# Level-zero products from the keys themselves, one product for the rows' first values, and a new order of the work

## The chip, the cores and the metric

The kernel runs on one core of a Trainium2 chip. The metric is the device time of one launch, in microseconds; three runs of the kernel before gave 5051.2 us in the median (5048.74 to 5053.33).

## The reference, cut to what matters

A macaron block: half a feed-forward layer, an attention-like layer with a delta rule, half a feed-forward layer again, each on normalised inputs and added to the input. The change touches the middle layer only, for 8 sequences of 256 tokens, 16 heads, 4 keys and values per token, chunks of 64 tokens in the reference:

```python
w = bg[..., None] * kg
Mi = [einsum('bhtsd,bhsmd->bhtsm', kg[:, :, :, i, :][:, :, :, None, :] * Dts, w) for i in range(Rr)]
M = tril(stack(Mi, axis=3).reshape(b, h, C * Rr, C * Rr), k=-1)
kexp = kg * exp(Gg)[:, :, :, None, :]
rhs = (vg - einsum('bhtid,bhdv->bhtiv', kexp, S)).reshape(...)
u = solve_triangular(M, rhs, lower=True, unit_diagonal=True)
o = SCALE * (o_inter + o_intra)          # from q exp(G) S and attn u
S_new = exp(glast)[..., None] * S + einsum('bhtid,bhtiv->bhdv', kdec, u)
```

Here `Dts` is exp of a difference of cumulated log decays, `kdec` the keys times the decay to the chunk's end. Keys, queries and values come from projections, a causal convolution of 4 taps and silu.

## The kernel before, in words

Everything is float32. After the first feed-forward phase come 64 head steps (4 tiles of 512 tokens, 16 heads); each holds two sequences' halves (`hb` 0 and 1) of 8 chunks `c` of 32 tokens with 4 keys each, 128 rows per chunk. The work of one head step is spread over about four turns of one loop: in turn `p` every engine works on steps `p+1` (projections), `p`, `p-1`, `p-2` (inverse and recurrence) and `p-3` (output). In the texts here `s0` is step `p`, `s1` is `p-1`, and so on, and `sn` is `p+1`. Each engine has its own list of calls, written out by hand, and runs it strictly in that order; a call first waits on semaphores that say its operands are there and its target is empty. PSUM banks 0 and 1 go round among projections, turns, norm, gate, decay and output (`bank_use`), the accumulators `acc` among the convolutions (`acc_use`).

The parts of a step:

- `project_k(s, 0..4)` (4 keys and the query) and `project_v(s, 0..3)` on TensorE; `tap_*` (ScalarE) and `conv_*` (VectorE, three taps) into `acc`; `silu_*` (ScalarE) into `KQ` and `V`. `decay`, `softplus`, `add_up` (a scan, L1437), `distance` and `factors` (ScalarE, exponentials F0, Fl, Fe) make the decay factors.
- `products(s, q, l)` for four groups `q` of 16 token blocks: the products of keys with keys and queries, split by level `l` of a binary tree so that the decay factors never overflow. `levels(s, q, l)` on VectorE (L1394) makes X = KQ times Fl for levels 1 to 4, `level(s, q)` on GpSimd (L1769, L1770) makes X0 for level 0: a copy of the 40 columns of KQ and 20 more columns times F0. All levels 0 to 2 of a group go to bank 2, levels 3 and 4 to bank 3. `evacuate` (VectorE, L1479 and L1485) empties bank 2 into Pd, `keep` (ScalarE) bank 3 into E and At.
- `take`, `norm`, `weigh` (VectorE) lay the first 32 by 32 blocks out; `begin` on GpSimd (L1778, L1784) clears LZ and puts the first values of the rows in with four instructions, `rows` (L1796, L1799) solves 31 rows by 62 instructions, each behind the one before. `unfold` and `turn` on VectorE, `first` to `fourth` on TensorE with copies on ScalarE join the blocks to the inverse Ztf.
- `spread` on GpSimd (L1739) makes kexp and kdec, `query` (L1758) qn; `turn` on TensorE (L810) transposes kdec, `turn_v` (L801) V.
- The recurrence over chunks, both halves interleaved: `rhs` on TensorE, `rhs` on VectorE (Rs, L1397), `solve` on TensorE, `solve` on ScalarE (Us), `update` on TensorE (kdT, At, qn), `update` on VectorE (S), and again. Then `out_square`, `mean_square`, `out_root`, `gated`, `output`.

All products go through one helper (L739), VectorE's through L1394 and L1397, ScalarE's through L1056 and L1057, so the trace is read by tiles.

Of the kernel before, what the change touches and what calls it, by code (L numbers as in the profile page):

```python
# [12 lines left out]
P = 128  # L13
# [13 lines left out]
C_SEL = C_SMALL + 6  # L27
# [64 lines left out]
def build(nc, x, out, wkq, wv, wo, vec, wf1, wg1, wb, bg1, wu, wd, fvec, wsd, cst, B, H):  # L92
# [4 lines left out]
    with ctx:  # L97
# [24 lines left out]
        half_c = [cs[:, C_SEL + 16 + half:C_SEL + 17 + half] for half in range(2)]  # L122
# [436 lines left out]
        X0 = sb("X0", [P, 16, 60])  # L559
# [16 lines left out]
        LZ = sb("LZ", [P, 32, 16])  # L576
# [35 lines left out]

        g_zero, g_kdec, g_kexp, g_qn, g_copy, g_X0, g_init, g_row = (sem(f"g_{n}") for n in ("zero", "kdec", "kexp", "qn", "copy", "X0", "init", "row"))

        def turns(order, count):
# [10 lines left out]
            ("k", 3, 0, v_ck, 15, 11), ("ms", 0, 3, a_ms, 3, 0), ("k", 4, 0, v_ck, 15, 14),  # L628
            ("gate", 0, 1, a_gate, 1, 0), ("out", 0, 3, v_out, 2, 0), ("v", 2, 1, v_cv, 12, 8),
            ("v", 3, 1, v_cv, 12, 11), ("out", 1, 3, v_out, 2, 1), ("vturn", 0, 2, a_vt, 4, 0),  # L630
            ("vturn", 1, 2, a_vt, 4, 1), ("turn", 0, 1, a_kdT, 4, 0), ("vturn", 2, 2, a_vt, 4, 2),
            ("vturn", 3, 2, a_vt, 4, 3), ("k", 0, -1, v_ck, 15, 2), ("norm", 0, 0, a_qs, 1, 0),
            ("turn", 1, 1, a_kdT, 4, 1), ("k", 1, -1, v_ck, 15, 5), ("k", 2, -1, v_ck, 15, 8),
            ("turn", 2, 1, a_kdT, 4, 2), ("turn", 3, 1, a_kdT, 4, 3), ("v", 0, 0, v_cv, 12, 2),
            ("decay", 0, -1, v_sp, 1, 0), ("v", 1, 0, v_cv, 12, 5),
        ], 2)
        acc_use = turns([
            ("k", 3, 0, a_k, 5, 3), ("k", 4, 0, a_k, 5, 4), ("v", 2, 1, a_v, 4, 2),
            ("v", 3, 1, a_v, 4, 3), ("k", 0, -1, a_k, 5, 0), ("k", 1, -1, a_k, 5, 1),
            ("k", 2, -1, a_k, 5, 2), ("v", 0, 0, a_v, 4, 0), ("v", 1, 0, a_v, 4, 1),  # L640
# [94 lines left out]
        def delta_tensor(e):  # L735
# [216 lines left out]
            for p in range(-1, NS + 3):  # L952
                project_k(p, 3)
                solve(p - 3, 1, 7)
                update(p - 3, 0, 7)
                update(p - 3, 1, 7)
                mean_square(p - 3)
# [10 lines left out]
                products(p - 1, 2, 0)  # L968
                products(p - 1, 2, 1)
                first(p - 2, 0)  # L970
                products(p - 1, 2, 2)
                second(p - 2, 0)
                products(p - 1, 2, 3)
                output(p - 3, 1)
# [5 lines left out]
                turn_v(p - 2, 2)  # L980
                products(p - 1, 2, 4)
                turn_v(p - 2, 3)
                first(p - 2, 1)
                project_k(p + 1, 0)
                second(p - 2, 1)
                products(p - 1, 3, 0)
                total(p)
# [4 lines left out]
                solve(p - 2, 0, 0)  # L992
                third(p - 2, 1)
                turn(p - 1, 1)
                update(p - 2, 0, 0)
                fourth(p - 2, 1)
                project_k(p + 1, 1)
                solve(p - 2, 1, 0)
                rhs(p - 2, 0, 1)
                project_k(p + 1, 2)  # L1000
# [4 lines left out]
                products(p, 0, 0)  # L1005
                rhs(p - 2, 0, 2)
                solve(p - 2, 1, 1)
                products(p, 0, 1)
                turn(p - 1, 2)
                solve(p - 2, 0, 2)  # L1010
                update(p - 2, 1, 1)
                rhs(p - 2, 1, 2)
                update(p - 2, 0, 2)
                products(p, 0, 2)
                solve(p - 2, 1, 2)
                rhs(p - 2, 0, 3)
                update(p - 2, 1, 2)
                solve(p - 2, 0, 3)
                rhs(p - 2, 1, 3)
                update(p - 2, 0, 3)  # L1020
                solve(p - 2, 1, 3)
                rhs(p - 2, 0, 4)
                update(p - 2, 1, 3)
                turn(p - 1, 3)
                solve(p - 2, 0, 4)
                project_v(p, 0)
                rhs(p - 2, 1, 4)
                update(p - 2, 0, 4)
                solve(p - 2, 1, 4)
                decay(p + 1)  # L1030
                rhs(p - 2, 0, 5)
                update(p - 2, 1, 4)
                products(p, 0, 3)
                solve(p - 2, 0, 5)
                rhs(p - 2, 1, 5)
                products(p, 0, 4)
                solve(p - 2, 1, 5)
                update(p - 2, 0, 5)
                rhs(p - 2, 0, 6)
                update(p - 2, 1, 5)  # L1040
                rhs(p - 2, 1, 6)
                solve(p - 2, 0, 6)
                solve(p - 2, 1, 6)
                update(p - 2, 0, 6)
                update(p - 2, 1, 6)
                rhs(p - 2, 0, 7)
                project_v(p, 1)
                solve(p - 2, 0, 7)
                rhs(p - 2, 1, 7)

        def delta_scalar(e):
# [252 lines left out]
            for p in range(-1, NS + 3):  # L1304
                silu_v(p - 1, 0)
                solve(p - 3, 1, 7)
                tap_k(p, 3)
                out_square(p - 3)
                e.preload_act_table_set("natural_log_exp_and_others")
# [15 lines left out]
                tap_v(p - 1, 3)
                first(p - 2, 0)
                second(p - 2, 0)
                silu_v(p - 1, 2)
                silu_k(p, 4)
                third(p - 2, 0)  # L1330
                turned_v(p - 2, 0)
                turned_v(p - 2, 1)
                square(p)
                turned(p - 1, 0)
                fourth(p - 2, 0)
                turned_v(p - 2, 2)
                turned_v(p - 2, 3)
                rhs(p - 2, 0, 0)
                silu_v(p - 1, 3)
                first(p - 2, 1)  # L1340
                keep(p - 1, 2)
                tap_k(p + 1, 0)
                second(p - 2, 1)
                e.preload_act_table_set("natural_log_exp_and_others")
                factors(p, 0)
                solve(p - 2, 0, 0)
                keep(p - 1, 3)
                third(p - 2, 1)
                turned(p - 1, 1)
                excess(p)  # L1350
                factors(p, 1)
                length(p - 1, 0)
                fourth(p - 2, 1)
                update(p - 2, 0, 0)
                rhs(p - 2, 1, 0)
                tap_k(p + 1, 1)
# [565 lines left out]
```

## Time and profile before

| | |
|---|---|
| median of three runs | 5051.2 us |
| profiled execution | 5064.96 us, its span 5063.2 us |
| TensorE busy | 4653.1 us, 92% |
| VectorE, ScalarE, GpSimd busy | 78%, 66%, 63% |
| mean granted clock of TensorE | 0.946 |
| matmuls | 63328 records (two for each float32 product) |

Busy time is how long at least one instruction of the engine was on its way; for TensorE the end of a product is modelled, and products overlap, so the time from one start to the next says more of its work than the busy share. A granted clock of 1.00 is 2.4 GHz, 0.50 is 1.2 GHz. In the rows, a bracket after a row gives the idle time of the engine ahead of it and what ended it. Weight loads have rows of their own (PEld).

### The profile page before, as it was taken

To read this page: it belongs to the slowest core of one execution; us is meant where nothing else is said; L and a number is where in the kernel's file an instruction comes from. 1 tells how busy PE (TensorE), PEld (TensorE's weight loads), DVE (VectorE), ACT (ScalarE), POOL (GpSimd) and SP (SyncE) were. 2 spreads that over 40 slices of the span, in tenths; PEclk is the share of its full clock that TensorE was granted. 3 is DMA by queue.
4 is the path that set the end of the run, shared out by engine and by line. 5 is a ranking of instruction groups with operands and counts; after the bars stand their busy time and mean duration, and the time that the engine had idled before them with its cause. 6 is when DMAs were issued, how large, how long until landed. Compare 5 with 4: busy or idle time off the path is not lost.

```text
span 5063.2 us, 151418 instructions
## 1 busy us (share of the span) xinstructions
PE 4653.1 (92%) x63328; PEld 3247.3 (64%) x63328; DVE 3967.3 (78%) x7070; ACT 3357.1 (66%) x6641; POOL 3179.8 (63%) x5380
## 2 busy tenths in 40 slices
PE   8869999999999999999999999999999999999889
PEld 5436666666666666666666666666666666666655
DVE  3278888888878888888888888888888888888522
ACT  2267777767767777767677767777677777677421
POOL 0047667767767676777667767677776677676600
PEclk9989999999999999999999999999999999999769
DMA  2110000000000000000100000000000000000010
GB/s 87 62 49 23 25 25 25 13 25 25 33 20 25 29 25 25 25 13 25 33 31 29 14 25 25 25 25 16 27 29 25 25 16 22 25 25 9 3 45 18
DMA packets 49722, 135.45 MB, mean 27 GB/s; under 512 B 7056, under 2 KB 28176, under 8 KB 48400
## 3 DMA queue, kind: packets, MB, share of 16 engines
q1 hardware_dynamic: 49040, 125.77, 7.1%
q8 instruction: 499, 8.18, 0.7%
q14 instruction: 183, 1.50, 0.1%
HBM read 111.60 MB, written 14.16 MB: 25 GB/s over the span
## 4 chain that ended last, share of the span: by engine, by line
PE 60%; DVE 25%; ACT 9%; issue 5%; POOL 1%; DMA 1%; SPq 0%; DVEq 0%; ACTq 0%
PE bank L739 50%; DVE X L1394 9%; PE bank L261 7%; DVE acc L1397 7%; ACT o L1057 2%; PE bank L810 2%; DVE S L1397 1%; DVE o L1397 1%; DVE Pd L1479 1%; DVE x1m L1394 1%; PE bank L801 1%; DVE Zc L1558 1%; DVE C L1437 1%; ACT Ztf L1056 1%; ACT Fl L1057 1%
## 5 line engine op out<-in xcount | busy, mean ns | idle before, releaser
L1397 DVE SCALAR_TENSOR_TENSOR acc<-bank,vc,acc 128x510 f32<-128x510 f32 (+2 forms) x1728 | 1272.3, 742 | 157.9 <-ACT acc L1056 134.9
L1799 POOL TENSOR_TENSOR LZ<-LZ,LT 128x120 f32<-128x120 f32 (+26 forms) x1984 | 958.4, 483 | 155.4
L1394 DVE TENSOR_TENSOR X<-KQ,Fl 128x640 f32<-128x640 f32 x1024 | 1011.4, 1013 | 15.2 <-ACT Fl L1057 15.1
L1796 POOL TENSOR_TENSOR LT<-LA,LZ 128x120 f32<-128x120 f32 (+26 forms) x1984 | 845.2, 426 | 145.8
L1056 ACT ACTIVATE Us<-bank 128x128 f32<-128x128 f32 x1024 | 282.2, 276 | 864.7 <-PE bank L739 852.4
L1769 POOL COPY X<-KQ 128x640 f32<-128x640 f32 x256 | 184.3, 720 | 993.6 <-ACT F L1057 664.8
L739 PEld LDWEIGHTS bank<-X 128*32 128x32 f32 x32768 | 535.9, 115 | 362.3 <-issue 219.8
L739 PE MATMUL bank<-X 128*32 128x60 f32 (+1 forms) x32768 | 648.4, 209 | 127.4 <-DVE Pd L1479 96.3
L739 PE MATMUL bank<-xnTm,WK 128*128 128x512 f32 x1280 | 658.9, 640 | 30.3 <-DMA WK<-in_wkq 13.8
L739 PE MATMUL bank<-xnTm,WV 128*128 128x512 f32 x1024 | 492.7, 605 | 10.6 <-DVE acc L1397 5.1
L739 PE MATMUL bank<-Rs,Ztf 128*128 128x128 f32 x2048 | 458.8, 306 | 36.4 <-ACT Rs L1056 18.3
L1397 DVE SCALAR_TENSOR_TENSOR Rs<-V,knT,bank 128x128 f32<-128x128 f32 x896 | 309.8, 346 | 215.7 <-PE bank L739 208.2
L1739 POOL TENSOR_TENSOR kdec<-KQ,Fe 128x512 f32<-128x512 f32 x256 | 353.4, 1380 | 197.9 <-PE bank L810 197.8
L739 PEld LDWEIGHTS bank<-Rs,Ztf 128*128 128x128 f32 x2048 | 328.3, 193 | 208.0 <-issue 74.1
L1056 ACT ACTIVATE acc<-bank,vc 128x512 f32<-128x512 f32 x576 | 393.8, 684 | 65.8 <-PE bank L739 62.5
L739 PE MATMUL bank<-S,kexp 128*128 128x128 f32 x1792 | 396.6, 304 | 21.9 <-DVE S L1397 0.8
L739 PE MATMUL bank<-Us,kdT 128*128 128x128 f32 x1792 | 384.6, 297 | 16.1
L739 PEld LDWEIGHTS bank<-xnTm,WK 128*128 128x128 f32 x1280 | 228.2, 198 | 266.0 <-issue 185.8
L1739 POOL TENSOR_TENSOR kexp<-KQ,Fe 128x512 f32<-128x512 f32 x256 | 382.0, 1503 | 0.0
L739 PEld LDWEIGHTS bank<-S,kexp 128*128 128x128 f32 x1792 | 283.9, 193 | 118.7 <-DVE S L1397 83.2
L739 PE MATMUL bank<-qn,S 128*128 128x32 f32 x1792 | 352.0, 279 | 0.0
L1397 DVE SCALAR_TENSOR_TENSOR S<-S,egl,bank 128x128 f32<-128x128 f32 x768 | 262.7, 342 | 96.5 <-PE bank L739 92.7
(145 smaller groups left out, 9341.0 us busy)
## 6 DMA issues: line engine op xcount, KB each, us to landing
WK<-in_wkq SPq DMA_DIRECT2D x64, 704.0 KB, 5.6
WV<-in_wv SPq DMA_DIRECT2D x64, 576.0 KB, 4.2
WO<-in_wo SPq DMA_DIRECT2D x64, 128.0 KB, 2.0
wuh<-in_wu SPq DMA_DIRECT2D x2, 1024.0 KB, 7.3
xt<-in_x SPq DMA_DIRECT2D x4, 512.0 KB, 6.4
wuh_d<-wuh SPq DMA_DIRECT2D x1, 2048.0 KB, 6.3
x_d<-x SPq DMA_DIRECT2D x4, 512.0 KB, 3.1
xnT_d<-xT SPq DMA_DIRECT2D x4, 512.0 KB, 2.7
```

What stands on the lines that cost most here:

```text
L261: return e.matmul(o, l, r, start=start, stop=stop, skip_group_check=True)
L739: return e.matmul(o, l, r, start=start, stop=stop, skip_group_check=True)
L801: ins = e.transpose(o[:, P * c:P * c + P], V[:, s % 2, 4 * q + c, :], ident)
L810: ins = e.transpose(o[:, P * c:P * c + P], kdec[:, c, :], ident)
L1056: return e.activation(o, i, f, scale=scale)
L1057: return e.activation(o, i, f, bias=bias, scale=scale)
L1394: return e.tensor_tensor(o, a, b, op)
L1397: return e.scalar_tensor_tensor(out=o, in0=a, scalar=sc, in1=b, op0=op0, op1=op1)
L1739: return e.tensor_tensor(o.rearrange("p u (g i t) -> p (u g) i t", g=4, i=R), KQ[:, s % 2, 16 * q:16 * q + 16, 0:R, :], f.unsqueeze(2).bro ...
L1769: e.tensor_copy(X0[:, :, 0:40], kk.rearrange("p g i t -> p g (i t)")).then_inc(g_copy, 1)
L1796: e.tensor_tensor(tmp, LA[:, j + 1:32, 8 * (j % R) + j // R].unsqueeze(2).broadcast_to([P, rr, cc]), LZ[:, j, 0:cc].unsqueeze(1).broadcast ...
L1799: e.tensor_tensor(LZ[:, j + 1:32, 0:cc], LZ[:, j + 1:32, 0:cc], tmp, SUB).then_inc(g_row, 1)
```

## The change

Three edits, and a new order on four engines.

1. `products(s, q, 0)` reads keys and queries from KQ: a product of the 32 key columns with the 40 columns of keys and queries, and one of the same keys with the 20 scaled columns of X0. X0 has 20 columns per block instead of 60, the copy in `level` goes, and `products` waits for silu of all five blocks.
2. `begin` writes the rows' first values with one instruction, through a view of LZ (`LZd`) and a product with a two-column mask.
3. The order of calls of all four engines is another one, with the bank and accumulator rounds that follow from it; the loop's start is cut at another place, so calls that stood at its end for `p-2` now stand at its start for `p-3`.

```diff
-        half_c = [cs[:, C_SEL + 16 + half:C_SEL + 17 + half] for half in range(2)]
+        half_c = cs[:, C_SEL + 16:C_SEL + 18]
...
-        X0 = sb("X0", [P, 16, 60])
+        X0 = sb("X0", [P, 16, 20])
...
-        LZ = sb("LZ", [P, 32, 16])
+        LZt = sb("LZ", [P, 8 * 66])
+        LZ = LZt[:, 0:512].rearrange("p (r c) -> p r c", c=16)
+        LZd = LZt[:, :].rearrange("p (t x) -> p t x", x=66)[:, :, 0:64].rearrange("p t (h y) -> p t h y", y=32)[:, :, :, 0:18:17]
...
                     w.wait_ge(a_E, nth(s, 8, 2 * q - 1))
+                    w.wait_ge(a_k, every(s, 5))
                     w.wait_ge(g_X0, nth(s, 4, q))
...
-                            ins = mm(o[:, 0:60], X0[:, gb + g, 0:32], X0[:, gb + g, :])
+                            kg = KQ[:, s % 2, 16 * q + gb + g]
+                            mm(o[:, 0:40], keys(kg), kg.rearrange("p i t -> p (i t)"))
+                            ins = mm(o[:, 40:60], keys(kg), X0[:, gb + g, :])
...
-                e.tensor_copy(X0[:, :, 0:40], kk.rearrange("p g i t -> p g (i t)")).then_inc(g_copy, 1)
-                e.tensor_tensor(X0[:, :, 40:60].rearrange("p g (i t) -> p g i t", t=4), kk[:, :, :, 1:8:2],
+                e.tensor_tensor(X0[:, :, :].rearrange("p g (i t) -> p g i t", t=4), kk[:, :, :, 1:8:2],
                                 f.unsqueeze(2).broadcast_to([P, 16, 5, 4]), MUL).then_inc(g_X0, 1)
...
-                flat = LZ[:, :, :].rearrange("p r c -> p (r c)")
-                for k in range(2):
-                    for hf in range(2):
-                        a = 32 * hf + 17 * k
-                        e.tensor_scalar(flat[:, a:a + 463:66], Cn[:, :, 2 * hf + k], half_c[hf], None,
-                                        MUL).then_inc(g_init, 1)
+                e.tensor_tensor(LZd, Cn[:, :, :].rearrange("p t (h k) -> p t h k", h=2),
+                                half_c.unsqueeze(1).unsqueeze(3).broadcast_to([P, 8, 2, 2]), MUL).then_inc(g_init, 1)
```

The new lists, shortened (one entry per call, `3,0` for arguments after the step; `update(s3,1,5)` is `update(p - 3, 1, 5)`).

```
TensorE: update(s3,1,5) solve(s3,0,6) project_k(s0,3) rhs(s3,1,6) update(s3,0,6) solve(s3,1,6) rhs(s3,0,7)
 update(s3,1,6) solve(s3,0,7) products(s1,0,3) rhs(s3,1,7) project_v(s1,1) solve(s3,1,7) update(s3,0,7)
 update(s3,1,7) products(s1,0,4) mean_square(s3) project_k(s0,4) products(s1,1,0..2) gate products(s1,1,3..4)
 output(s3,0) project_v(s1,2) project_v(s1,3) products(s1,2,0) first(s2,0) products(s1,2,1..2) second(s2,0)
 output(s3,1) products(s1,2,3) third(s2,0) turn_v(0) turn_v(1) fourth(s2,0) turn(s1,0) turn_v(2) first(s2,1)
 turn_v(3) products(s1,2,4) second(s2,1) total(s0) project_k(sn,0) solve(s2,0,0) products(s1,3,0..4) turn(s1,1)
 third(s2,1) project_k(sn,1) update(s2,0,0) fourth(s2,1) rhs(0,1) turn(s1,2) solve(1,0) solve(0,1) update(1,0)
 update(0,1) rhs(1,1) project_k(sn,2) rhs(0,2) solve(1,1) solve(0,2) update(1,1) update(0,2) rhs(1,2) rhs(0,3)
 solve(1,2) solve(0,3) update(1,2) products(s0,0,0) rhs(1,3) update(0,3) turn(s1,3) rhs(0,4) solve(1,3)
 project_v(s0,0) products(s0,0,1) solve(0,4) update(1,3) update(0,4) rhs(1,4) decay(sn) rhs(0,5) solve(1,4)
 solve(0,5) update(1,4) products(s0,0,2) rhs(1,5) update(0,5) solve(1,5) rhs(0,6)
VectorE: rhs(s3,0,6) update(1,5) softplus(s0) rhs(1,6) update(0,6) levels(s1,1,1) rhs(0,7) update(1,6) conv_k(s0,3,2)
 levels(s1,1,2) rhs(s3,1,7) conv_k(3,1) conv_k(3,0) levels(s1,1,3) conv_v(1,2) conv_v(1,1) evacuate(s1,0,0)
 conv_v(1,0) evacuate(0,1) levels(1,4) evacuate(0,2) evacuate(0,3) lengths gated(0) gated(1) conv_k(4,2..0)
 evacuate(1,0) unfold(0) unfold(1) evacuate(1,1) turn evacuate(1,2) output(s3,0) evacuate(1,3) levels(2,1..3)
 conv_v(2,2..0) conv_v(3,2..0) output(s3,1) add_up(s0) levels(2,4) levels(3,1) levels(3,2) evacuate(2,0)
 evacuate(2,1) levels(3,3) evacuate(2,2) distance(1) evacuate(2,3) levels(3,4) distance(2) conv_k(sn,0,2)
 conv_k(0,1) evacuate(3,0) conv_k(0,0) evacuate(3,1..3) take conv_k(1,2) norm(0) conv_k(1,1) rhs(s2,0,1) norm(1)
 conv_k(1,0) norm(2) weigh distance(3) ... (recurrence with conv_k(sn,2), levels(s0,0,.), conv_v(s0,0))
GpSimd: begin(s2) rows(s2,0) rows(4) level(s1,1) rows(8) .. rows(28) spread(s1,0,0) spread(0,1) level(s1,2) level(s1,3)
 spread(1,1) query(s1) spread(2,1) spread(1,0) spread(3,1) spread(2,0) level(s0,0) spread(3,0)
```

(`spread(q,0)` makes kdec, `spread(q,1)` kexp.) Before, GpSimd's list after `begin` was `rows(0)`, `rows(4)`, `spread(3,0)`, `rows(8)`, `level(1)`, `rows(12)` to `rows(28)`, `level(2)`, and so on; TensorE had `products(3,0..4)` ahead of the first `solve`, `products(0,4)` inside the recurrence; VectorE had `levels(2,4)`, `(3,1)`, `(3,2)`, `(3,3)` in a row, then three evacuations, `add_up`, `levels(3,4)` and the fourth evacuation. ScalarE's list changes in the same way; `silu_k(sn,0)` moves ahead of `factors(3)`, and there are four calls that load the table of exponentials in a turn instead of three.

## Rows read from the trace of the kernel before

**Rows 1.** The page: busy us and shares, and the chain that ended last.
```profile
PE 4653.1 (92%) x63328; PEld 3247.3 (64%) x63328; DVE 3967.3 (78%) x7070; ACT 3357.1 (66%) x6641; POOL 3179.8 (63%) x5380
...
PE 60%; DVE 25%; ACT 9%; issue 5%; POOL 1%; DMA 1%; SPq 0%; DVEq 0%; ACTq 0%
```
**Rows 2.** Scan L1437 (first, last start); windows: us, busy PE PEld DVE ACT POOL, PEclk.
```profile
L1437 DVE TENSOR_TENSOR_SCAN C<-cs,sp_t x64: 1212/1217/1400, 275.3 to 4674.9; 128x512 f32<-128x512 f32 x64
...
2081.02:2148.99 67.97, 63.32 (x970) 45.12 (x970) 60.75 (x108) 50.40 (x102) 50.48 (x84) 1.00 0.07 24
...
676.00:680.00 4.00, 3.71 (x101) 2.05 (x103) 3.02 (x6) 2.08 (x4) 1.44 (x2) 0.57 0.00 0
```
**Rows 3.** TensorE in order of time: start us, us, instruction; work by start to start.
```profile
2096.18 0.63 PE L739 MATMUL bank<-X 128*32 128x60 f32 x32
2096.74 0.49 PE L739 MATMUL bank<-S,kexp 128*128 128x128 f32 x2
...
2100.31 0.45 PE L739 MATMUL bank<-X 128*32 128x20 f32 x32
2100.69 0.49 PE L739 MATMUL bank<-Rs,Ztf 128*128 128x128 f32 x2
...
2117.56 1.88 PE L739 MATMUL bank<-xnTm,WV 128*128 128x512 f32 x4
2119.28 0.39 PE L739 MATMUL bank<-Rs,Ztf 128*128 128x128 f32 x2
2119.50 0.39 PE L739 MATMUL bank<-S,kexp 128*128 128x128 f32 x2
...
2127.90 2.03 PE L739 MATMUL bank<-X 128*32 128x60 f32 x128 [0.19 <-issue]
2129.86 1.13 PE L739 MATMUL bank<-fgm,WV 128*128 128x512 f32 x2
```
**Rows 4.** Windows of the two stretches of one step, columns as in rows 2.
```profile
2086.26:2122.65 36.39, 35.30 (x345) 27.30 (x342) 30.37 (x63) 24.29 (x53) 29.56 (x54) 1.00 0.01 2
2122.65:2154.23 31.58, 28.02 (x547) 17.11 (x549) 29.47 (x45) 26.13 (x49) 20.91 (x32) 0.95 0.14 49
```
**Rows 5.** TensorE in order of time: its waits in the second stretch.
```profile
676.29 1.03 PE L739 MATMUL bank<-X 128*32 128x60 f32 x32 [2.15 <-DVE Pd L1479]
...
2083.15 0.63 PE L739 MATMUL bank<-X 128*32 128x60 f32 x32 [2.16 <-DVE Pd L1479]
...
2123.60 1.10 PE L739 MATMUL bank<-o,cs 128*128 128x512 f32 x2 [0.78 <-ACT o L1057]
```
**Rows 6.** VectorE in order of time; the last row is all `levels` (min/median/max ns).
```profile
2066.13 2.27 DVE L1394 TENSOR_TENSOR X<-KQ,Fl 128x640 f32<-128x640 f32 x3
2068.34 4.53 DVE L1397 SCALAR_TENSOR_TENSOR acc<-bank,vc,acc 128x510 f32<-128x510 f32 x6
...
2073.51 6.69 DVE L1394 TENSOR_TENSOR X<-KQ,Fl 128x640 f32<-128x640 f32 x4
...
2080.48 0.71 DVE L1479 COPY_PREDICATED Pd<-cs,bank 128x80 f32<-128x80 uint32 x2
...
L1394 DVE TENSOR_TENSOR X<-KQ,Fl x992: 782/818/1902, 327.5 to 4672.2; 128x640 f32<-128x640 f32 x199
```
**Rows 7.** GpSimd in order of time.
```profile
2074.01 3.69 POOL L1739 TENSOR_TENSOR kexp<-KQ,Fe 128x512 f32<-128x512 f32 x2
...
2085.05 0.72 POOL L1769 COPY X<-KQ 128x640 f32<-128x640 f32 x1 [5.54 <-ACT F L1057]
...
2088.50 1.27 POOL L1739 TENSOR_TENSOR kdec<-KQ,Fe 128x512 f32<-128x512 f32 x1 [1.57 <-PE bank L810]
...
2092.26 2.81 POOL L1784 TENSOR_SCALAR LZ<-Cn,cs 128x8 f32<-128x8 f32 x4
2095.16 0.25 POOL L1796 TENSOR_TENSOR LT<-LA,LZ 128x31 f32<-128x31 f32 x1
```
**Rows 8.** ScalarE in order of time: one table load.
```profile
2082.29 1.28 ACT L1344 ACT_TABLE_LOAD   x1
```

More of the change, by code:

```diff
@@ L611, in build @@
         v_Rs, v_S, v_o, v_out = (sem(f"v_{n}") for n in ("Rs", "S", "o", "out"))
-        g_zero, g_kdec, g_kexp, g_qn, g_copy, g_X0, g_init, g_row = (sem(f"g_{n}") for n in ("zero", "kdec", "kexp", "qn", "copy", "X0", "init", "row"))
+        g_zero, g_kdec, g_kexp, g_qn, g_X0, g_init, g_row = (sem(f"g_{n}") for n in ("zero", "kdec", "kexp", "qn", "X0", "init", "row"))
         def turns(order, count):
@@ L952, in delta_tensor @@
             for p in range(-1, NS + 3):
+                update(p - 3, 1, 5)
+                solve(p - 3, 0, 6)
                 project_k(p, 3)
+                rhs(p - 3, 1, 6)
+                update(p - 3, 0, 6)
+                solve(p - 3, 1, 6)
+                rhs(p - 3, 0, 7)
+                update(p - 3, 1, 6)
+                solve(p - 3, 0, 7)
+                products(p - 1, 0, 3)
+                rhs(p - 3, 1, 7)
+                project_v(p - 1, 1)
                 solve(p - 3, 1, 7)
@@ L980, in delta_tensor @@
                 turn_v(p - 2, 2)
+                first(p - 2, 1)
+                turn_v(p - 2, 3)
                 products(p - 1, 2, 4)
-                turn_v(p - 2, 3)
-                first(p - 2, 1)
+                second(p - 2, 1)
+                total(p)
                 project_k(p + 1, 0)
-                second(p - 2, 1)
+                solve(p - 2, 0, 0)
                 products(p - 1, 3, 0)
-                total(p)
                 products(p - 1, 3, 1)
@@ L1623, in delta_vector @@
             for p in range(-1, NS + 3):
+                rhs(p - 3, 0, 6)
+                update(p - 3, 1, 5)
+                softplus(p)
+                rhs(p - 3, 1, 6)
+                update(p - 3, 0, 6)
+                levels(p - 1, 1, 1)
+                rhs(p - 3, 0, 7)
+                update(p - 3, 1, 6)
+                conv_k(p, 3, 2)
+                levels(p - 1, 1, 2)
+                rhs(p - 3, 1, 7)
+                conv_k(p, 3, 1)
+                conv_k(p, 3, 0)
+                levels(p - 1, 1, 3)
                 conv_v(p - 1, 1, 2)
                 conv_v(p - 1, 1, 1)
+                evacuate(p - 1, 0, 0)
+                conv_v(p - 1, 1, 0)
+                evacuate(p - 1, 0, 1)
+                levels(p - 1, 1, 4)
                 evacuate(p - 1, 0, 2)
-                conv_v(p - 1, 1, 0)
-                conv_k(p, 3, 2)
-                conv_k(p, 3, 1)
                 evacuate(p - 1, 0, 3)
-                conv_k(p, 3, 0)
-                levels(p - 1, 1, 4)
+                lengths(p - 2)
                 gated(p - 3, 0)
@@ L1700, in delta_vector @@
-                conv_k(p + 1, 2, 1)
-                update(p - 2, 0, 3)
-                conv_k(p + 1, 2, 0)
+                conv_k(p + 1, 2, 1)
+                update(p - 2, 0, 2)
+                rhs(p - 2, 1, 2)
+                rhs(p - 2, 0, 3)
+                conv_k(p + 1, 2, 0)
+                update(p - 2, 1, 2)
+                levels(p, 0, 1)
+                rhs(p - 2, 1, 3)
+                update(p - 2, 0, 3)
+                diagonal(p - 1)
+                distance(p, 4)
+                levels(p, 0, 2)
@@ L1728, in delta_vector @@
-                levels(p, 1, 3)
-                rhs(p - 2, 1, 7)
+                levels(p, 0, 4)
         def delta_gpsimd(e):
@@ L1803, in delta_gpsimd @@
             for p in range(-1, NS + 3):
+                begin(p - 2)
+                rows(p - 2, 0)
+                rows(p - 2, 4)
+                level(p - 1, 1)
+                rows(p - 2, 8)
+                rows(p - 2, 12)
                 rows(p - 2, 16)
```

242 lines of the change are left out of this document (102 added, 140 removed).

## The prediction

> **What bounds the kernel now.** I read the page first, then the time between two steps, then TensorE's instructions over one step, and then who holds the operand wherever they stop. The page puts 92% of the span on TensorE and 60% of the chain that ended last on PE, 25% on DVE [rows 1]. The scan of `add_up` runs once per head step: 64 of them from 275.3 to 4674.9 us are 63 intervals of 4399.6 / 63 = 69.8 us [rows 2]. So the delta phase makes about 4.5 of the 5.06 ms, and a microsecond per step is worth 64 us, or 1.3%. A step at full clock takes 67.97 us (granted clock 1.00) [rows 2]. On average 69.8 - 68.0 = 1.9 us per step is the clock's, at its lower level of 1.2 GHz. In 676 to 680 us the granted clock was 0.57, and the first product in it, at 676.29, had waited 2.15 us for VectorE [rows 2, 5]; that place of the step returns below.
>
> TensorE's work in one full-clock step, from start to next start where nothing is waited for [rows 3]: 9 projections at 1.72 (as from 2117.56 to 2119.28) = 15.5; 58 small products of the recurrence (`rhs`, `solve`, and in `update` kdT and qn) at 0.22 = 12.8; 16 products with At at 0.14 = 2.2; 4 groups of `products`, 2.3 each (1.96 for all five levels in a stream at 2127.90, more where a level stands alone: 0.56 for level 0, 0.38 for level 1) = 9.4; 8 turns at 0.5 = 4; `first` to `fourth`, twice, at 1.07 for the large ones and 0.6 for the small = 6.6; decay, gate, total at 0.9 = 2.7; mean square and output = 3.7. Sum 56.9. So 67.97 - 56.9 = 11.1 us of a step are waits of TensorE. The page's busy time hides most of them, since the modelled end of one product covers the wait of the next.
>
> The step falls into two stretches [rows 4]. From the first `solve` to the last `update` (the recurrence) 36.39 us hold 30.4 of that work, so 6 are waits, nearly all too short for the trace to name: each round of a chunk goes TensorE, VectorE, TensorE, ScalarE, TensorE, VectorE, and its operand comes just in time or 0.1 to 0.5 us late. From there to the next first `solve` 31.58 us hold 26.5, so 5.1 are waits. The largest has a name: 2.16 us until `evacuate` frees bank 2 ahead of `products(3,0)`; then 0.78 for `out_square` [rows 5].
>
> Why is VectorE late at 2083? Four `levels` took 6.69 us at 2073.5; three of them alone took 2.27 at 2066.1, and the median of all is 818 ns against a maximum of 1902 [rows 6]. In the same stretch GpSimd ran kexp and kdec, 3.69 us for two that take 1.28 at other times [rows 7]. Unhindered the four need 4 x 0.75 = 3.0, so 3.7 us are lost to the two engines standing in each other's way, and VectorE reaches the evacuation that much later.
>
> **The change part by part.** *Level 0 split.* Per group of `products(.,0)`, 16 products of 60 columns (32 records) become 16 of 40 and 16 of 20 (64 records). The trace has no stream of 40-column products on four column groups. Standing alone, 60 columns took 0.56 us (2096.18 to 2096.74) and 20 columns 0.38 [rows 3]. Below: the columns are the same, 0 more. Above: a whole 20-column product beside a 60-column one, 0.38 more. Between: 40 columns at (0.56 + 0.38) / 2 = 0.47, so 0.47 + 0.38 - 0.56 = 0.29, less a little since the two follow each other in one stream (five levels in a stream took 1.96 where the single ones add up to more): I take 0.25, four times per step +1.0 us (0 to +1.5). I count it in full, since three of the four stand where TensorE does not wait for long. The added wait for `a_k` costs nothing: silu of block 4 ends a third of a step ahead of the first group; behind it on TensorE would stand the whole recurrence.
> The Trainium skill ("TensorE: Matmul & The Clock Gate", section "Wait — 56ns, not 53.3ns?") says that starts of matmuls never come closer than about 25 ns however few columns they have. By that the 32 added records would cost 0.8 us, 3.2 per step. The rows speak against it here: 32 records of 20 columns start within 0.38 us, 12 ns each [rows 3]. It is rival C.
>
> *GpSimd.* The copy of 720 ns goes, four times a step: -2.9 us. In `begin`, four instructions (2.81 us with VectorE beside them) become one; the nearest row is a product of 31 elements at 0.25, so -1.4 to -2.5 [rows 7]. GpSimd waited 5.54 us for the factors in this one step, so its own time is not the bound. The gain lies in its chain from `begin` to the last `rows`: without what is moved out or shortened (`spread(3,0)` 1.27, a copy 0.72, `begin` 2) it is 4 us shorter. The unfolding on VectorE follows right behind it and keeps its place behind `gated` and `conv_k(4,.)`, so this is cover and not gain.
>
> *ScalarE.* One table load more (before `factors(3)`, since `silu_k(0)` now stands ahead of it), perhaps a second at the loop's start: 1.28 each [rows 8]. ScalarE is busy 50.4 of 68 us [rows 2]. Its load before `factors(3)` stands ahead of `solve(1,3)`, so that `Us` may come up to 1.3 late once; with 2.0 us of `project_v(0)`, `update` and `turn` between, I count 0, at most +0.6.
>
> *The new order, second stretch.* I follow it from the last `update` (t = 0) with the durations above; a convolution tap counts 0.75 and an evacuation 0.3 [rows 6]. `out_square` needs ScalarE until 0.9, `mean_square` starts there as now; `project_k(4)`; `products(1,0)` waits for `evacuate(0,3)`, which VectorE reaches at 4.4, when TensorE also does; `output(0)` waits 0.3 for `conv_k(4,0)`; `project_v(3)` waits 0.8 for the bank of `output(0)`, which stands behind both unfolds and `turn` on VectorE; `first`, `second`, `third` and the turns wait 0.9 together for ScalarE. Then comes the place of the 2.16. In both orders TensorE has about 3.5 us of other work between `products(2,4)`, which completes bank 2, and `products(3,0)`, which needs it empty. VectorE's part now starts only after four slowed `levels`, 2.7 us after that product ended, and has the scan and a `levels` inside it [rows 5, 6]. In the new order `add_up`, `levels(2,4)`, `(3,1)` and `(3,2)` stand ahead, while GpSimd waits for `turn(0)`, and after them 0.3 + 0.3 + 0.75 + 0.3 + 0.6 + 0.25 = 2.5 us (evacuations, one `levels`, `distance(1)`): no wait at bank 2. Waits in all 0.3 + 0.8 + 0.9 and 0.3 for small ones = 2.3 instead of 5.1.
>
> *The recurrence.* `products(3,.)` of 2.3 us move into its head and `products(0,4)` of 0.7 leaves it, so its work is 30.4 + 1.6 + 0.5 (two split groups) = 32.5. Followed the same way with VectorE and ScalarE free, its waits are 3.3. But VectorE has 30 us of its own work in these 33 (three convolutions of keys, `take` 2.2, `weigh` 1.2, six `levels`, 26 steps of 0.27), and each `Rs` queues behind what stands before it. I therefore leave the waits at the 6 of now; the ends are 3.3 and 9.5 (a half microsecond more in each of 7 rounds).
>
> **The sum.** Work 56.9 + 1.0 = 57.9; waits 2.3 + 6 = 8.3; a full-clock step 66.2, or 1.8 less than 67.97. With the same 1.9 us of lower clock per step, 64 x 1.8 = 115 us. The profiled execution took 5064.96 us, 13.8 above the median of 5051.2: 5064.96 - 115 - 13.8 = 4936; rounded with the ScalarE and GpSimd trifles, which I put at nothing, to 4935.
>
> **The rivals.** *A, slower: VectorE bounds the recurrence.* If `Rs` and `S` wait so often that the waits there exceed 6 + 1.8 = 7.8 us, the step is as long as now; at 9.5 it is 69.7 and the time 5051 + 64 x 1.7 = 5160; at the middle, 8.8, 5115. For it: VectorE is 90% full there, and the second `rhs` now stands behind `take` and two convolutions. Against: VectorE was busy 30.4 of 36.4 us in this stretch before, and the waits were short [rows 4].
> *B, the clock holds.* The wait at bank 2 stands where the clock fell. Without it, and with waits of 3.3, the step is 63.5, and half of the 1.9 us comes back: 64 x (4.5 + 0.9) = 345 less at most, 4710; half of it, 4850, is the case I weigh.
> *C, starts bound level 0.* 3.2 instead of 1.0 per step: 64 x 2.2 = 141 above the forecast, 5075, slower than now.
> *D, nothing moves.* The two engines meet elsewhere (rows of GpSimd beside `levels(0,.)` and `(1,.)`, now as before), the wait at bank 2 is made good by one at another bank, and the 1.0 of level 0 cancels what is left: 5050.
>
> **How the numbers follow.** Forecast (4880 to 5000) 0.50, B 0.23, A 0.16, C 0.03, D 0.08. A measurement here can tell 0.2%, 10 us, from no change. Faster: 0.50 + 0.23 and a quarter of D, 0.75; same 0.06; slower 0.19. The range takes in most of B and the mild end of D: 4800 to 5060.
>
> **What would show it.** Right: `products` with 64 records of 40 and 20 columns per group, 0.6 to 0.7 us; no wait over 1 us for Pd; median and mean of `levels` within 10% of each other; full-clock steps near 66. Wrong: TensorE waiting for `Rs`, `S` or for a bank by more than 8.5 us per step; level 0 groups near 1.2 us (C); a granted clock below 0.95 between 326 and 4675 us.

## The result, and the profile after

| | before | after |
|---|---|---|
| median, us | 5050.0 | 5213.3 |
| ratio to before, 95% interval | | 1.0328 (1.0293 to 1.0364) |
| profiled execution and its span, us | 5064.96; 5063.2 | 5217.37; 5215.6 |
| mean step (63 intervals of the scan), us | 69.8 | 72.3 |
| shortest step at full clock, us | 67.98 | 66.94 |
| mean less shortest, us | 1.9 | 5.4 |

The change made the kernel 3.3% slower. The page of the kernel after: busy us, the instruction queue (packets, MB, share), and the chain that ended last.
```profile
PE 4801.7 (92%) x71520; PEld 3383.0 (65%) x71520; DVE 3803.5 (73%) x7070; ACT 3456.0 (66%) x6709; POOL 2828.6 (54%) x4932
...
q8 instruction: 563, 9.22, 0.7%
...
PE 62%; ACT 17%; DVE 13%; issue 7%; POOL 1%; DMA 0%; SPq 0%; DVEq 0%; ACTq 0%; POOLq 0%
```
The same queue on the page of the kernel before:
```profile
q8 instruction: 499, 8.18, 0.7%
```
Against [rows 1] VectorE fell from 25% of the chain to 13%, and GpSimd is busy 351 us less; TensorE has 8192 more records of products (two for each product) and as many more weight loads. Keep the queue's 64 additional packets in mind.

The scan of the kernel after (all 64), then two windows (us, busy PE PEld DVE ACT POOL, PEclk): the shortest step without a fall of the clock, from one `total` on TensorE to the next, and the whole phase.
```profile
L1443 DVE TENSOR_TENSOR_SCAN C<-cs,sp_t x64: 1214/1215/2084, 275.5 to 4833.1; 128x512 f32<-128x512 f32 x64
```
```profile
3758.40:3825.34 66.94, 64.47 (x1106) 46.45 (x1099) 57.23 (x107) 51.64 (x102) 44.33 (x77) 1.00 0.08 28
322.27:4833.10 4510.83, 4204.97 (x67761) 3003.73 (x67761) 3551.83 (x6543) 3201.60 (x6287) 2746.24 (x4775) 0.95 0.07 23
```
(4833.1 - 275.5) / 63 = 72.3 us per step, 2.5 more than in [rows 2], though the undisturbed step is 1.0 shorter. So everything that was lost lies between the undisturbed step and the mean one. What ends TensorE's waits (us in total, times, longest, from 322 to 4650 us), kernel after and kernel before:
```profile
PE bank L741 <- issue: 117.3, 96, 2.6
PE bank L741 <- ACT Us L1061: 72.8, 58, 1.3
PE bank L741 <- DVE Rs L1403: 30.8, 120, 0.3
PE bank L741 <- DVE acc L1403: 20.3, 53, 2.4
```
```profile
PE bank L739 <- DVE Pd L1479: 91.4, 46, 2.5
PE bank L739 <- ACT o L1057: 47.4, 61, 0.8
PE bank L739 <- issue: 41.5, 75, 2.2
```
The waits for bank 2 (Pd) and for `o` are gone, as the new order meant them to be. The wait for `Us` is new; a table load makes it (below). `issue`, a wait for nothing that the profile shows, has nearly tripled. Of the 19 steps of the kernel after that ran at full clock throughout, the seven without such a wait of over 0.25 us took 66.9 to 67.2 us, the other twelve 68.1 to 71.2. One such wait in the kernel after, TensorE in order of time, and around it five windows:
```profile
1699.37 0.60 PE L741 MATMUL bank<-X 128*32 128x20 f32 x46
1702.22 1.33 PE L741 MATMUL bank<-X 128*32 128x20 f32 x45 [2.25 <-issue]
...
1704.52 1.97 PE L741 MATMUL bank<-Zc,E 64*64 64x64 f32 x16
...
1710.35 1.14 PE L741 MATMUL bank<-Ztf,Y 64*64 64x64 f32 x16
```
```profile
1694.00:1698.00 4.00, 3.29 (x60) 1.77 (x54) 2.71 (x7) 2.46 (x7) 0.52 (x1) 1.00 0.13 51
1698.00:1702.00 4.00, 1.97 (x119) 1.56 (x117) 2.52 (x4) 3.86 (x8) 0.00 (x0) 1.00 0.02 6
1702.00:1706.00 4.00, 3.78 (x63) 3.23 (x64) 2.30 (x6) 0.62 (x2) 1.32 (x2) 0.62 0.02 4
1706.00:1710.00 4.00, 4.00 (x10) 1.91 (x9) 1.67 (x1) 1.82 (x4) 0.66 (x1) 0.53 0.00 0
1710.00:1714.00 4.00, 4.00 (x40) 3.57 (x38) 3.15 (x8) 3.34 (x10) 1.46 (x2) 1.00 0.00 0
```
This is group 3. TensorE stops with about half of the records of levels 1 to 4 done, between two products of one level, where no semaphore is waited for; then the granted clock falls to the lower level, 1.2 GHz. The 16 records of `third` take 1.97 us in it, the 16 of the same size of `fourth` 1.14 when the clock is back. What arrives during the stop is an instruction packet. DMA of the same 6 us, in 40 slices of 0.15 us:
```profile
GB/s 55 0 0 0 0 0 0 0 0 0 0 0 0 109 0 0 0 0 0 0 0 0 0 0 0 0 0 0 0 0 0 0 0 0 0 109 0 0 0 0
...
q8 instruction: 2, 0.03, 2.3%
```
A packet of 16 KB started at 1700.0 us (the median one takes 1.06); TensorE went on at 1702.22. The trace has 86 such stops of over 0.4 us, 48 of them inside a group of `products` and nearly all others among the narrow products of `first` to `third`. After them TensorE restarted 1.2 to 1.5 us (tenth to ninetieth percentile) behind the landing of such a packet; from a random moment back to the last packet it is 1 to 11 us. The queue grows with TensorE's instructions: 8192 more records and 8192 more weight loads brought 64 more packets of 16 KB, 64 bytes for each instruction, and in the experiments below half of the split brings 32 packets more and a quarter 16. So `issue` is here TensorE out of instructions.

The falls of the clock have such a stop, or another wait, ahead of them. I took for each of the 68 falls in the last 61 steps of the kernel after the longest wait of TensorE in the 6 us before: it is a nameless stop at 42 of them and the wait for `Us` at 26. In the median TensorE had waited 1.4 us in those 6, against 0.15 before a random moment. In group 3, whose products are the same in every step, the clock fell in 23 of the 33 steps with a stop of over 1 us there, and in none of the other 28.

### The profile page after: what moved, and what is told of

It is laid out like the page before. It is cut to its first block, busy times and chain, and to the rows that moved or that the text cites. A ratio compares the mean times of both kernels' runs of the same rounds, so it can differ in the third digit from the quotient of the medians.

```text
span 5215.6 us, 167423 instructions
## 1 busy us (share of the span) xinstructions
PE 4801.7 (92%) x71520; PEld 3383.0 (65%) x71520; DVE 3803.5 (73%) x7070; ACT 3456.0 (66%) x6709; POOL 2828.6 (54%) x4932
## 4 chain that ended last, share of the span: by engine, by line
PE 62%; ACT 17%; DVE 13%; issue 7%; POOL 1%; DMA 0%; SPq 0%; DVEq 0%; ACTq 0%; POOLq 0%
PE bank L741 49%; PE bank L261 7%; DVE acc L1403 4%; PE bank L803 3%; ACT Ztf L1061 3%; ACT acc L1061 2%; PE bank L812 2%; ACT L1310 2%; DVE Rs L1403 2%; ACT L1062 2%; DVE X L1400 1%; DVE o L1403 1%; ACT rn L1062 1%; ACT o L1062 1%; ACT L1323 1%
## 5 line engine op out<-in xcount | busy, mean ns | idle before, releaser
L1800 POOL TENSOR_TENSOR LZ<-LZ,LT 128x120 f32<-128x120 f32 (+26 forms) x1984 | 940.4, 474 | 155.5
L1797 POOL TENSOR_TENSOR LT<-LA,LZ 128x120 f32<-128x120 f32 (+26 forms) x1984 | 890.8, 449 | 150.7 <-POOL LZ L1785 0.3
L1745 POOL TENSOR_TENSOR kdec<-KQ,Fe 128x512 f32<-128x512 f32 x256 | 327.5, 1279 | 1120.0 <-PE bank L812 1106.2
L1400 DVE TENSOR_TENSOR X<-KQ,Fl 128x640 f32<-128x640 f32 x1024 | 854.5, 855 | 0.0
L741 PE MATMUL bank<-X 128*32 128x20 f32 x24576 | 522.5, 203 | 89.9 <-issue 82.0
L741 PEld LDWEIGHTS bank<-X 128*32 128x32 f32 x24576 | 423.3, 113 | 251.5 <-issue 223.1
L1775 POOL TENSOR_TENSOR X<-KQ,F 128x320 f32<-128x320 f32 x256 | 195.2, 763 | 682.8 <-PE bank L741 397.2
L741 PE MATMUL bank<-xnTm,WV 128*128 128x512 f32 x1024 | 521.4, 638 | 5.9 <-DVE acc L1403 2.7
L741 PE MATMUL bank<-Rs,Ztf 128*128 128x128 f32 x2048 | 469.0, 313 | 40.7 <-DVE Rs L1403 33.8
L741 PE MATMUL bank<-Us,kdT 128*128 128x128 f32 x1792 | 400.0, 306 | 85.4 <-ACT Us L1061 77.0
L741 PEld LDWEIGHTS bank<-Us,kdT 128*128 128x128 f32 x1792 | 281.8, 195 | 158.5 <-ACT Us L1061 113.9
```

The costliest lines, as they stand in the source:

```text
L741: return e.matmul(o, l, r, start=start, stop=stop, skip_group_check=True)
L1400: return e.tensor_tensor(o, a, b, op)
L1745: return e.tensor_tensor(o.rearrange("p u (g i t) -> p (u g) i t", g=4, i=R), KQ[:, s % 2, 16 * q:16 * q + 16, 0:R, :], f.unsqueeze(2).bro ...
L1775: e.tensor_tensor(X0[:, :, :].rearrange("p g (i t) -> p g i t", t=4), kk[:, :, :, 1:8:2], f.unsqueeze(2).broadcast_to([P, 16, 5, 4]), MUL) ...
L1797: e.tensor_tensor(tmp, LA[:, j + 1:32, 8 * (j % R) + j // R].unsqueeze(2).broadcast_to([P, rr, cc]), LZ[:, j, 0:cc].unsqueeze(1).broadcast ...
L1800: e.tensor_tensor(LZ[:, j + 1:32, 0:cc], LZ[:, j + 1:32, 0:cc], tmp, SUB).then_inc(g_row, 1)
```

## Experiments: which part lost the time

Each was timed beside the kernel before, whose median was 5046 to 5056 us there; the ratio is to it. "Falls" are falls of the granted clock to the lower level; time at the lower level is (1 - mean clock) x 2 x span.

**The rows' first values alone, in the old order.**
```diff
-                for k in range(2):
-                    for hf in range(2):
-                        e.tensor_scalar(flat[:, a:a + 463:66], Cn[:, :, 2 * hf + k], half_c[hf], None, MUL)
+                e.tensor_tensor(LZd, Cn[...], half_c..., MUL)
```


> The kernel before with the one-instruction begin alone, level 0 and order as before. By theory S the whole loss of e1 is the split: 5030 to 5065 us. If GpSimd's earlier end moves collisions with VectorE: 5100 or more.


Measured 5048.9, ratio 0.9999 (0.9982 to 1.0015). GpSimd's begin is under cover, as predicted.

**The old order with both edits.** The kernel before with edits 1 and 2.


> The old order of all engines with the two code edits (level 0 split, one instruction in begin). Theory O, the order and the clock that goes with it cost the time: TensorE gets 0.9 us of work more per step, GpSimd 3.5 us less; time 5020 to 5090 us, granted clock as before. Theory L, the split of level 0 costs it: 5150 to 5210.


Measured 5210.3, 1.0320 (1.0286 to 1.0354): the whole loss without the new order, so theory L. TensorE's wait for Pd is 33.0 us in it instead of 91.4, `issue` 106.0 instead of 41.5.

**The new order with level 0 as before.**
```diff
-                            mm(o[:, 0:40], keys(kg), kg.rearrange("p i t -> p (i t)"))
-                            ins = mm(o[:, 40:60], keys(kg), X0[:, gb + g, :])
+                            ins = mm(o[:, 0:60], X0[:, gb + g, 0:32], X0[:, gb + g, :])
...
+                e.tensor_copy(X0[:, :, 0:40], ...)
```


> The new order, with level 0 as before (one product of 60 columns from X0, copy on GpSimd). Theory O: still slower than before by 2% or more, 5140 to 5190 us. Theory L: 5010 to 5070.


Measured 5009.8, 0.9920 (0.9899 to 0.9942): theory L. Its shortest step is 66.68 us, the mean 69.0.

**The same, with TensorE's split alone.**
```diff
-                            ins = mm(o[:, 0:60], X0[:, gb + g, 0:32], X0[:, gb + g, :])
+                            mm(o[:, 0:40], X0[:, gb + g, 0:32], X0[:, gb + g, 0:40])
+                            ins = mm(o[:, 40:60], X0[:, gb + g, 0:32], X0[:, gb + g, 40:60])
```


> As e2, but level 0 in two products of 40 and 20 columns, both from X0, and the copy stays: only TensorE's instructions differ from e2. Theory S, splitting the product is what costs (TensorE's work by 0.9 us a step, and the clock): 5150 to 5230 us, level 0 groups of 0.75 us, clock 0.94. Theory Q, reading keys and queries from KQ or GpSimd's earlier start costs: 5000 to 5080.


Measured 5242.2, 1.0401 (1.0341 to 1.0462): theory S, and 12 us more than its range. The same columns are read from the same tile with the same waits; only the number of products (and of the weight loads that go with them) differs, and 232 us are lost. The shortest step grows by 0.5 us only. Spans and mean clocks, whole and split:
```profile
core 0: 5009.7 us, clock 0.956
```
```profile
core 0: 5250.1 us, clock 0.937
```
and TensorE's waits in each (322 to 4650 us):
```profile
PE bank L741 <- issue: 37.7, 35, 2.3
```
```profile
PE bank L741 <- issue: 110.8, 91, 2.6
```
So of the 240 us between the profiled spans 73 are stops for instructions. Time at the lower clock rose from 441 to 661 us; at half the speed such a microsecond costs TensorE half a microsecond where nothing covers it, so I estimate 110 at most. The longer step gives 0.5 x 63 = 31. Some 25 us stay without a name. In group 3, 32 of 61 steps have a stop of over 1 us with the split, 25 of them with a fall behind it; with level 0 whole it is 11 and 8.

**More columns without more products.** Each product streams 100 columns instead of 60; the 40 behind are overwritten by the next products.
```diff
-                            ins = mm(o[:, 0:60], X0[:, gb + g, 0:32], X0[:, gb + g, :])
+                            c0, nc0 = 60 * (gb + g), 100 if gb + g < 15 else 60
+                            ins = mm(o[:, 0:nc0], X0[:, gb + g, 0:32], X0[...][:, c0:c0 + nc0])
```


> As e2, but one product of 100 columns instead of 60 in 15 of 16 blocks (columns 60 to 99 are junk that levels 1 and 2 overwrite): as long on TensorE as the split, with the old number of weight loads and products. Theory D, it is the sparseness of many short products that lets the clock fall: the group takes about 0.75 us as in after, but the clock stays as in e2, time 5030 to 5090. Theory W, any 0.2 us more per group does it: 5150 to 5230.


Measured 5036.9, 0.9985 (0.9955 to 1.0016): 27 us more than whole, 205 less than split, though a group takes TensorE as long as a split one (0.64 us from the first start to the last, against 0.61 to 0.67 split and 0.41 whole). `issue` is 30.9 us. What costs is not TensorE's time but the number of short instructions.

**More columns in the split.** The kernel after, its second product with 60 columns instead of 20.
```diff
-                            ins = mm(o[:, 40:60], keys(kg), X0[:, gb + g, :])
+                            c0, nc0 = 20 * (gb + g), 60 if gb + g < 14 else 20
+                            ins = mm(o[:, 40:40 + nc0], keys(kg), X0[...][:, c0:c0 + nc0])
```


> After, with the second product of level 0 at 60 columns instead of 20 in 14 of 16 blocks (the 40 more are junk that levels 1 and 2 overwrite): the same 64 records and weight loads per group, 100 columns through the array instead of 60. Theory D1, what holds the clock is how many columns stream per time: time falls though TensorE does more, 5040 to 5150 us, and the clock rises above 0.945. Theory D2, the number of short products and weight loads lets it fall: as after or slower, 5210 to 5300.


Measured 5157.0, 1.0268 (1.0187 to 1.0348): more work, and the median is 56 us below after, but the two intervals overlap, so the times alone show no gain; it lies between the two theories. `issue` fell from 117.3 to 88.2 us, which fits a product that lasts longer and so gives the next instructions time to come.

**Where the split costs.** The kernel with level 0 whole, split in some of the groups (`if q == 3`, `if q < 2`, `if q == 2`).


> The new order with level 0 read from X0, whole (one product of 60 columns) in groups 0 to 2 and split (40 and 20 columns) in group 3 alone, whose five levels follow each other in one stream. Whole everywhere gave 5010, split everywhere 5242. Theory I, TensorE runs out of instructions: stops of over 0.25 us between two products of the same group, where no semaphore is waited for, summed to 126 us with the split and 40 without, and lie mostly behind group 3; so splitting group 3 alone brings half or more of the 232 us, 5120 to 5180, with 60 to 100 us of such stops. Theory II, each narrow product costs the same clock wherever it stands: a quarter, 5068, stops as without the split.


Measured 5074.4, 1.0054 (1.0028 to 1.0080). Stops of over 0.25 us between narrow products of one kind came to 65 us, against 40 with all whole, some 50 of them 4 to 8 us into a step, in group 3. Theory I had the stops right and the time too high, theory II the time right and the stops wrong.


> The same with groups 0 and 1 split and groups 2 and 3 whole; group 0 stands in the recurrence, between large products, group 1 between projections and mean square. Theory I: no more stops than without the split, so only the direct 2 x 0.2 us x 64 = 26 us, 5030 to 5050. Theory II: half of 232, 5126.


Measured 5029.1, 0.9960 (0.9933 to 0.9987), `issue` 36.2 us: theory I. Groups 0 and 1, between projections, cost 19 us, no more than the shortest step shows (67.15 against 66.68, 30 us); the intervals of this run and of the one with all whole overlap.


> As the run with group 3 split alone, but group 2 is split alone; its level 0 stands at the end of the step, ahead of first, second, third and the turns. Splitting group 3 alone cost 64 us, groups 0 and 1 together 19, all four 232. If each place has its own price, group 2 has the rest, 149 us: 5160, with the long falls of the clock 62 to 68 us into a step that the kernel with all four split has in a third of its steps and the whole one seldom. If a group's price is a quarter wherever it stands, 5068. If the groups only cost that much together (each fall brings the next), about as group 3 alone, 5050 to 5090.


Measured 5079.8, 1.0062 (1.0041 to 1.0084), `issue` 69.7 us. So 19 + 64 + 70 = 153 of the 232 us belong to places, mostly those where the narrow products of groups 2 and 3 stand beside others (`first` to `third`, the turns); the other 79 are lost only where all four are split (by the intervals of the five runs I estimate this rest to within some 45 us).

**Time for the instructions to come.** The kernel after, with four products of a constant inside group 3, into columns that nothing reads.
```diff
                 products(p - 1, 3, 0)
+                for _ in range(4): mm(bank[2][:, 400:512], ident, cs[:, C_ONE:C_ONE + 112])
                 products(p - 1, 3, 1)
```


> The kernel after with four more products of 112 columns (a constant, into columns of bank 2 that nothing reads) between products(3,0) and products(3,1): 16 more instructions and about 0.85 us of dense work per step, 54 us if nothing else changes. Theory I: the stops behind group 3 (74 us in 58 steps) shrink to under 30, since the instructions have time to arrive, and the falls of the clock 6 to 9 us into a step become rare: 5080 to 5170. Theory II: the stops are nothing to the clock, which falls for the narrow products behind group 3; they are still there: 5200 to 5270.


Measured 5197.0, 1.0288 (1.0233 to 1.0342). The stops in group 3 shrank from some 74 to some 37 us, and of 59 steps 50 instead of 26 spent no time at the lower clock between `total` and `decay`; no fall begins there, where the kernel after has 24 in 61 steps. Mean less shortest step went from 5.4 to 3.8 us. But the shortest step grew by 1.3 (68.28), not 0.85, which took 84 of the 100 us back. On the cause this is for theory I, on the time nearer to II, and the interval overlaps that of after: what is gained the filler eats. It does not part the two effects of a filler, though: in 18 steps a stop of over 1 us still stands in group 3, and no fall follows.

## Experiments: the table load and the clock

**Without the table load at the loop's start.**
```diff
             for p in range(-1, NS + 3):
-                e.preload_act_table_set("natural_log_exp_and_others")
                 decay(p, 2)
```


> After, without the table load at the loop's start (the table is there already). Theory T, the two loads on ScalarE ahead of Us in round 6 make TensorE wait and the clock fall there: 50 to 130 us less, 5080 to 5165, and the clock falls less often between decay and mean square. Theory V, VectorE's queue sets the recurrence: less than 15 us of difference.


Measured 5045.9, 0.9989 (0.9965 to 1.0014): 167 us less than after, theory T with more than its range. ScalarE in the kernel after, in order of time:
```profile
2097.51 1.28 ACT L1310 ACT_TABLE_LOAD   x1
2098.80 0.72 ACT L1062 ACTIVATE rn<-rn,cs 128x512 f32<-128x512 f32 x1
2099.43 0.26 ACT L1061 ACTIVATE Us<-bank 128x128 f32<-128x128 f32 x1
2099.71 1.28 ACT L1062 ACT_TABLE_LOAD   x1
2101.00 0.63 ACT L1062 ACTIVATE KQ<-acc 128x512 f32<-128x512 f32 x1
2101.73 0.69 ACT L1061 ACTIVATE acc<-bank,vc 128x512 f32<-128x512 f32 x1
2102.31 0.27 ACT L1061 ACTIVATE Us<-bank 128x128 f32<-128x128 f32 x1
```
and TensorE meanwhile:
```profile
2100.97 0.49 PE L741 MATMUL bank<-Rs,Ztf 128*128 128x128 f32 x2 [0.29 <-DVE Rs L1403]
...
2102.63 0.49 PE L741 MATMUL bank<-Us,kdT 128*128 128x128 f32 x2 [0.92 <-ACT Us L1061]
```
Without the call the exponential behind it (`rn`) takes no load of its own, so the table was there already; the call loads it again. TensorE's wait for `Us` is gone from the list of its waits, while `issue` stays at 120.4 us. The shortest step is 1.21 us shorter (65.73), 76 us in 63 steps; and between `decay` and mean square, behind this wait, none of 59 steps has a fall (24 had one), so that the mean is 3.8 instead of 5.4 above the shortest, 101 us.

**Both: level 0 whole and no second load.**


> The new order with level 0 as before (as e2) and without the table load at the loop's start (as e3). If the two costs add up, step by step, 2.2 us per step (1.2 of work and 1.0 of the clock) leave e2: 4850 to 4900 us. If both were only the same falls of the clock counted twice: 4980 to 5030.


Measured 4911.5 (4902.6 to 4924.1), 0.9736 (0.9708 to 0.9763), the fastest of all, and 12 us above the range for two costs that add up. Span and clock, its scan, and its shortest step:
```profile
core 0: 4901.4 us, clock 0.963
```
```profile
L1440 DVE TENSOR_TENSOR_SCAN C<-cs,sp_t x64: 1211/1215/1644, 274.3 to 4512.1; 128x512 f32<-128x512 f32 x64
```
```profile
3785.10:3850.67 65.57, 63.41 (x977) 45.34 (x970) 57.49 (x107) 50.12 (x101) 48.77 (x82) 1.00 0.08 24
```
67.3 us per step, 1.7 above the shortest: what the prediction was made of, with the old level 0.

**Filler at the waits of the recurrence.** The kernel after with eight products of 128 columns per step.
```diff
+            def fill(s): mm(bank[4][:, 0:128], ident, ones)
```


> After, with eight extra products of 128 columns per step (ident times ones, into bank 4, which nobody needs then; 0.22 us each) at the waits of TensorE in the recurrence. Theory K, the clock falls because TensorE is too little busy there: fewer falls in the recurrence, mean granted clock 0.95 or more, time 5080 to 5150. Theory V, the waits come from the chain between engines and the clock matters little: the fillers add 0 to 100 us, 5210 to 5310.


Measured 5128.9, 1.0153 (1.0115 to 1.0191): 84 us less, with 1.8 us more work per step; `issue` stays (108.8 us). The falls between `decay` and mean square went.

**A projection into the stream of group 3.** `project_k(p + 1, 1)` from behind `third` to between `products(p - 1, 3, 0)` and `(3, 1)`, in the kernel after and in the fastest one.
```diff
                 products(p - 1, 3, 0)
+                project_k(p + 1, 1)
                 products(p - 1, 3, 1)
...
                 third(p - 2, 1)
-                project_k(p + 1, 1)
```


> After, with project_k(1) of the next step moved from behind third to between products(3,0) and products(3,1) (and the bank round to match). Theory K, the clock falls behind long runs of narrow products: the falls at 6 to 8 us after total go, cold time from total to decay halves, 5100 to 5170 us. Theory V, the waits are the chain's: 5195 to 5235.

> As e5 (new order, level 0 as before, no table load at the loop's start) with the same move of project_k(1). In e5 the clock falls hardly ever from total to decay (0.4 us per step), so by theory K little is left to win: 4890 to 4930 us; if the move itself shortens a wait: under 4890.


Measured 5548.9, 1.1010 (1.0961 to 1.1059), and 5307.9, 1.0523 (1.0481 to 1.0564): 336 and 396 us slower. I had the sign wrong, and neither theory named such a loss. Span and clock of the first:
```profile
core 0: 5536.2 us, clock 0.901
```
`issue` is down to 40.7 us, yet the clock falls 10 to 17 us into every step. What went wrong is new waits: the projection now takes its bank ahead of `turn(1)`, and two turns of each step wait until VectorE's convolutions have emptied theirs. From TensorE's waits (322 to 4650 us; the kernel after has no such rows), then one step in order of time, and two windows:
```profile
PE bank L812 <- DVE acc L1403: 159.6, 112, 4.7
PE bank L741 <- ACT S L1061: 38.9, 54, 1.1
```
```profile
2599.73 0.66 PE L812 MATMUL bank<-cs,kdec 128*128 128x128 f32 x4 [1.09 <-DVE acc L1403]
...
2604.36 0.46 PE L741 MATMUL bank<-S,kexp 128*128 128x128 f32 x2 [1.08 <-ACT S L1061]
2606.75 1.11 PE L812 MATMUL bank<-cs,kdec 128*128 128x128 f32 x4 [1.93 <-DVE acc L1403]
```
```profile
2603.00:2606.70 3.70, 0.74 (x7) 0.44 (x5) 2.61 (x7) 2.77 (x8) 0.00 (x0) 1.00 0.00 0
2606.70:2610.10 3.40, 3.35 (x15) 3.11 (x15) 3.03 (x3) 0.83 (x3) 1.99 (x4) 0.50 0.00 0
```
So these runs say nothing against stops as the cause: the 61 falls ahead of `decay` all stand behind such waits of TensorE, mostly for VectorE, and not behind a stop for instructions. What a wide product in the middle of group 3 does by itself they do not show.

## Why the prediction was wrong, step by step

- **The step that failed: "With the same 1.9 us of lower clock per step".** It was 5.4, which is 3.5 of the 4.2 us between the forecast mean step of 66.2 + 1.9 = 68.1 and the measured 72.3. By [rows 2] I took the whole distance between the mean and the shortest step for a constant of the clock. It holds the stops for instructions too, 41.5 us / 62 steps = 0.7 before and 117.3 / 60 = 2.0 after; the remaining 1.2 and 3.4 go, by difference, with the lower clock. The split moved both. Level 0 whole leaves 2.3, split from the same tile 5.7.
- **Level 0, "+1.0 us per step".** The shortest step shows 0.5, so as TensorE's time it was priced well enough: level 0 of one group runs from 2120.66 to 2121.31, 0.65 us, where the whole one takes 0.41. The instructions themselves were not in the sum.
- **ScalarE, "I count 0, at most +0.6".** Mis-sized: 1.2 in the shortest step, 167 us in all. I gave the load ahead of `factors(3)` a cover and did not follow the one at the loop's start, which stands ahead of two `Us` of round 6.
- **The second stretch, waits 5.1 to 2.3.** Right in its main term. VectorE now waits for TensorE at bank 2, and `levels` no longer pile up (median 819 ns, mean 855; before, mean 1013 on the page):
```profile
2059.59 2.27 DVE L1400 TENSOR_TENSOR X<-KQ,Fl 128x640 f32<-128x640 f32 x3
...
2064.32 0.34 DVE L1491 COPY_PREDICATED Pd<-cs,bank 128x160 f32<-128x160 uint32 x1 [2.47 <-PE bank L741]
```
- **The recurrence, waits left at 6, and the full-clock step of 66.2.** 66.94 with the second load, 65.73 without: right within its ends as far as the step tells; the waits inside the recurrence were not measured by themselves.
- **GpSimd, nothing.** Right: 0.9999.
- **Rival A** had nearly the time (5160), by luck, and not the reason: waits for `Rs` are 30.8 us in all, 0.5 per step. **B** went the other way: the wait at bank 2 is gone, and the time at the lower clock rose from 547 to 647 us. **C** named the right edit and the wrong price: 64 records of a group start within 0.65 us, 10 ns each, where C named 1.2 us; but more instructions was the right thing to be afraid of. **D** fell: with level 0 whole the order gains 0.8%, without the second load 2.6%.

One sign of being wrong came true, if narrowly: the granted clock between 326 and 4675 us is 0.947. The chance of 0.19 for slower was too low: none of the cases asked what the mean step has above the shortest one, though 2.8% of the time lay there. Two sums were off without moving the forecast: four groups of `products` at 2.3 us are 9.2 and not 9.4, and half of rival B's 345 us gives 4880 and not 4850.

## What to carry to other kernels

Split the mean into the undisturbed step and the rest before pricing an edit, and ask of the rest what makes it; here the undisturbed step got better, and the rest tripled. Count instructions as well as their time: many short products in a row ran the engine dry here, and many of the stops were followed by a lower clock, so the price was paid twice. Before moving a call, ask which bank it takes and who then waits for that bank. The version to keep is the new order with level 0 in one product from X0 and without the table load at the loop's start: 4911.5 us, 0.9736 (0.9708 to 0.9763) of before.

## What the runs showed of the hardware that I had not expected

- TensorE runs out of instructions: stops of up to 2.6 us inside a group, each of those over 0.25 us ended less than 2 us after a 16 KB packet of the instruction queue had landed, mostly 1.2 to 1.5 us.
- The clock fell behind waits of TensorE, whatever it waited for: instructions in the run without the second load (the longest wait before all 28 falls is a nameless stop), `Us` or instructions in the kernel after, a bank at VectorE with the projection moved. Not each stop brings a fall: of the 33 steps with one of over 1 us in group 3, 10 had none.
- A table load for a table that is already there is carried out, at 1.28 us.
- The same time at the lower clock costs differently by place: from scan to scan 6.0 us of it per step went with 1.2 us lost before, and 8.0 with 3.4 after. That before it met stretches in which TensorE waited for VectorE anyway would explain this, and is not shown.
